# Graph keys at a stride of 32 rows: V placed by copies, silu from the exponential

## Chip, cores and metric

The kernel runs on one core of a Trainium2 chip. The metric is the device time of one execution in microseconds (us). Engines: PE multiplies matrices (PEld is its weight load), DVE, ACT and POOL work on 128 partitions by element, SP only issues transfers. Everything is float32.

## What is computed

32 batches of 32 tokens of 128 features go through a transformer layer with modulation from a condition, and then through a graph attention layer in two directions. Cut to what matters:

```python
cmod = silu(c) @ w_ada + b_ada                     # 6 vectors of 128 for each batch
x_mod = ln(x) * (1 + scale_msa) + shift_msa
k, q, v = split(x_mod @ w_qkv)                     # 16 heads of 8
y = softmax((q / 8) @ k.T) @ v
x = x + gate_msa * (y @ w_proj + b_proj)
x = x + gate_mlp * (gelu(ln_mod(x) @ w_mlp1 + b_mlp1) @ w_mlp2 + b_mlp2)
# the graph layer: 32 queries, but only the first 20 tokens as keys
self_feat = concat(x, c or 0) @ W_self.T + b_self
for d in range(2):                                 # the adjacency as it is, and swapped
    A = adj if d == 0 else swapaxes(adj, 1, 2)
    aff = q1[d] @ k1[d].T / sqrt(8)                # masked by A.sum(-1) > 0
    w = softmax(aff + A @ w_bias + b_bias)         # over 20 keys, 16 heads
    output += (w @ self_feat[:, :20]) through Wout[d] + bout[d]
out = x + relu(self_feat + output)
```

## The kernel before

The kernel is a list of steps, `ORDER`, each a pair of stage and key. `ON` gives each its engine and `BANKS` each PSUM tile its bank of four (`ps_b0` to `ps_b3`); the scores have four banks of their own (`ps_s`). Each engine runs its steps in the list's order (`mine`), and before each waits for the steps that it needs (`fresh`). The order stands in the file as a table, and a step that waits holds back all behind it on its engine.

A unit is a group of four batches (128 query rows) and, in the graph layer, a direction: 8 units in the first layer, 16 in the graph layer. Sets of one or two units share softmax steps (`SETS`); the graph layer has eight sets of two (sets 5 to 12). The dense products go by chunks (`CHUNKS`, first layer up to the attention) or by four mids of eight batches (`MIDS`). A set passes through these stages:

- `scores` (L1030, PE): for each batch and each of four row strips j of the features a product of 32 queries with four heads' keys. K stands in `Kb0` or `Kb1` once for each of the four heads of a strip, masked by `head_mask` (`take` of k on ACT, L1101; `k1mask`, L755, on POOL or DVE, into a ring of two mids).
- `badd` (L1355, DVE, graph layer alone): adds the edge bias, PSUM to `E1`. `max` and `sub`: the row maximum of each head, and its subtraction (L1379 on DVE in the first layer, L723 on DVE or POOL in the graph layer). `E0` has a ring of two, `E1` of three sets.
- `turn` (L1041 graph, L1044 first layer, PE): transposes E of a unit, so that keys stand on partitions. The graph layer has 16 x 20 = 320 key columns, padded to 360 with -30000 by the step `zero pad`, in three parts of six heads x 20 keys (120 rows). The first layer has 16 x 32 = 512 columns in four parts of 128.
- `exp` (L1173 or L1176, ACT): exp from PSUM into `PT`, a ring of four units.
- `values` (L1066 or L1074, PE): for each part and batch a product of `PT` with V. V is block-diagonal: in `Vz1` a head's 20 rows hold its 8 columns and a column of ones (which yields the denominator), the rest zeros. `recip` and `mult` (L1388, L1399, DVE) divide. `ya` adds the two directions, `oT` turns back, `fin1`, `fin2` and `store` end the work.

V of the graph layer comes from the product `v1` (L989: only the 20 key rows of each batch) and a DVE transposition of 32 x 32 blocks (L1262) into `v1_raw`, where the keys of four heads stand at partitions 0, 32, 64 and 96. From there `spread_half` (L779) moves them by DMA to partitions at a stride of 20: 8 transfers a mid, 32 in all, 20 issued by SP and 12 by ACT. In the first layer `vmask` (L745) builds `Vz0` by multiplying with `quad_mask`.

The start: x is loaded in three parts, statistics on DVE (L1200, L1203), with epsilon added in L1206, the power -1/2 on POOL (L855), the scaled x on ACT or DVE (`apply`), its transposition on PE (`xnT`) and the modulation on DVE and POOL (`take` xnT and `shift`). `silu` (L1137) is one ACT step, after which the table for exp is loaded; the first `cmod` product waits for it and for its weights. PE runs 11 transpositions of `ident` first (`WARM`) and pairs of them in three `warm` steps.

Of the kernel before, what the change touches and what calls it, by code (L numbers as in the profile page):

```python
# [5 lines left out]
ALU = mybir.AluOpType  # L6
# [5 lines left out]
P = 128  # L12
B = 32
# [11 lines left out]
SIX = 6  # L25
CH = 3
CW = C + 1
UW = H * CW
KR = SIX * M
EW = CH * KR  # L30
# [21 lines left out]
SPREAD_PARTS = [[(0, 0, 0, 0, CH), (1, 1, 0, 0, CH), (4, 0, CH, 0, 1), (4, 1, CH, 1, 1)],  # L52
                [(2, 2, 0, 0, CH), (3, 3, 0, 0, CH), (5, 2, CH, 0, 1), (5, 3, CH, 1, 1)]]

# [16 lines left out]
WARM = 11  # L71
# [4 lines left out]
 'bhead': 'pool',  # L76
# [6 lines left out]
 'fin2': 'dve',  # L83
 'gbias': 'dve',
 'ident': 'pool',
 'k1mask': 'pool',
# [14 lines left out]
 'spread': 'sp',  # L101
 'stats': 'dve',
 'store': 'sp',
 'sub': 'pool',
 'turn': 'pe',
 'values': 'pe',
 'vmask': 'pool',
 'warm': 'pe',
 'ya': 'pool',
 'zero': 'pool',  # L110
 ('apply', 0): 'dve',
 ('bhead', 0): 'act',
 ('k1mask', (0, 1)): 'dve',
 ('k1mask', (1, 1)): 'dve',
 ('resid1', 2): 'dve',
 ('resid1', 3): 'dve',
 ('resid2', 2): 'pool',
 ('shift', (0, 0)): 'dve',
 ('shift', (0, 2)): 'dve',
 ('shift', (1, 2)): 'dve',  # L120
 ('spread', ('v1', 1, 0)): 'act',
 ('spread', ('v1', 2, 1)): 'act',
 ('spread', ('v1', 3, 1)): 'act',
 ('sub', 0): 'dve',
 ('sub', 1): 'dve',
 ('sub', 2): 'dve',
 ('sub', 3): 'dve',
 ('sub', 4): 'dve',
 ('sub', 7): 'dve',
 ('take', (('cmod', 0), 0)): 'dve',  # L130
 ('take', (('cmod', 1), 0)): 'dve',
 ('take', (('k', 0), 0)): 'act',
# [19 lines left out]
 ('take', (('k1', 0, 0), 0)): 'act',  # L152
 ('take', (('k1', 0, 1), 0)): 'act',
 ('take', (('k1', 1, 0), 0)): 'dve',
 ('take', (('k1', 1, 1), 0)): 'dve',
 ('take', (('k1', 2, 0), 0)): 'dve',
 ('take', (('k1', 2, 1), 0)): 'act',
 ('take', (('k1', 3, 0), 0)): 'act',
 ('take', (('k1', 3, 1), 0)): 'dve',
# [31 lines left out]
 ('take', (('q1', 1, 0), 0)): 'dve',  # L191
# [88 lines left out]
 ('turn', 12): 0,  # L280
# [1182 lines left out]
```

## Time and profile before

| what | us |
|---|---|
| median of 3 runs | 95.89 |
| lowest, highest | 95.29, 96.32 |
| the profiled execution | 96.85 |
| its span, first to last instruction | 95.1 |

Busy of the span are PE 87%, weight loads 69%, DVE 75%, POOL 52% and ACT 44%. The whole has 4068 recorded instructions, of which 1773 are PE products and transpositions and as many are weight loads: a float32 product is recorded as two products and two loads, a transposition as one of each. "Issue" in the chain or as a releaser is time in which an engine waited for nothing that the profile shows. The mean granted clock of PE is 0.982.

### The profile page before, as it was taken

The numbers are of one execution on the slowest core, as the hardware profiler recorded it, in microseconds if no ns is written. First come the engines' busy times: TensorE is split into PE (matmuls) and PEld (weight loads), VectorE is DVE, ScalarE is ACT, GpSimd is POOL, SyncE is SP. The second block draws the span as 40 slices with busy tenths as digits, with TensorE's granted clock in tenths as the row PEclk, the third lists the DMA queues.
The fourth block names the chain that finished last, engine by engine and source line by source line (L and its number), as shares of the span: only waits on it lengthen the run. The fifth ranks groups of instructions, "written<-read, shape, count | busy, mean of one in ns | idle before, by whom it ended". The sixth has DMA issues, their size and how long they took to land.

```text
span 95.1 us, 4068 instructions
## 1 busy us (share of the span) xinstructions
PE 82.7 (87%) x1773; PEld 65.6 (69%) x1773; DVE 71.7 (75%) x181; ACT 41.8 (44%) x96; POOL 49.0 (52%) x60
## 2 busy tenths in 40 slices
PE   3867999799999698999999999999999874998910
PEld 3745789567666386888878788788788763787700
DVE  3397477978796986888875999869788953689790
ACT  0928424977820488617066028731254221307300
POOL 4252439999976423239720541044995918263310
PEclk9999999999999999999999999999999999759999
DMA  1899991000000000000001100001110030020303
GB/s 35 263 317 277 422 405 64 0 0 7 3 7 7 0 3 7 0 0 0 7 0 30 38 10 0 7 0 21 24 41 8 16 70 6 21 57 16 110 7 110
DMA packets 3890, 5.75 MB, mean 60 GB/s; under 512 B 704, under 2 KB 3008, under 8 KB 3744
## 3 DMA queue, kind: packets, MB, share of 16 engines
q1 hardware_dynamic: 2840, 4.68, 15.3%
q10 hardware_dynamic: 1032, 0.80, 2.9%
q8 instruction: 14, 0.23, 1.0%
q14 instruction: 4, 0.03, 0.1%
HBM read 4.22 MB, written 0.52 MB: 50 GB/s over the span
## 4 chain that ended last, share of the span: by engine, by line
PE 74%; DVE 7%; issue 7%; ACT 4%; DMA 3%; POOL 1%; POOLq 1%; SPq 0%; ACTq 0%
PE ps_s L1030 12%; PE ps_b L971 7%; PE ps_b L945 7%; PE ps_b L965 7%; PE ps_b L894 5%; PE ps_b L1041 5%; PE ps_b L1066 5%; PE ps_b L1044 4%; PE ps_b L982 4%; PE ps_b L978 4%; DMA w_ada_sb<-in_w_ada 3%; PE ps_b L984 3%; PE ps_b L1074 2%; PE ps_b L921 2%; PE ps_b L953 2%
## 5 line engine op out<-in xcount | busy, mean ns | idle before, releaser
L1173 ACT ACTIVATE PT<-ps_b 120x384 f32<-120x384 f32 x16 | 7.2, 489 | 15.0 <-PE ps_b L1041 15.0
L755 POOL TENSOR_TENSOR Kb<-k_raw,head_mask 128x640 f32<-128x640 f32 x6 | 7.7, 1293 | 9.1 <-DVE k_raw L1273 4.7
L855 POOL TENSOR_TENSOR rstd<-var_eps,minus_half 128x2 f32<-128x2 f32 (+1 forms) x9 | 6.0, 671 | 8.6 <-DVE var_eps L1206 8.5
L723 POOL TENSOR_TENSOR E<-E,neg_max 128x640 f32<-128x640 f32 x7 | 8.9, 1271 | 0.9 <-DVE neg_max L1363 0.8
L1116 ACT ACTIVATE hidden<-ps_b,cols 128x256 f32<-128x256 f32 x16 | 7.1, 476 | 4.7 <-PE ps_b L965 4.7
L945 PE MATMUL ps_b<-xm,w_qkv_sb 128*128 128x256 f32 (+1 forms) x30 | 8.6, 418 | 0.0
L965 PE MATMUL ps_b<-xm,w_rest_sb 128*128 128x256 f32 x32 | 8.4, 381 | 0.0
L1066 PE MATMUL ps_b<-Vz,PT 120*32 120x54 f32 (+1 forms) x384 | 6.6, 216 | 2.1 <-issue 2.1
L1066 PEld LDWEIGHTS ps_b<-Vz,PT 120*32 120x32 f32 (+1 forms) x384 | 5.5, 116 | 4.0 <-issue 3.4
L1101 ACT ACTIVATE Kb<-ps_b,head_mask 128x256 f32<-128x256 f32 (+1 forms) x20 | 7.3, 440 | 1.9 <-PE ps_b L945 1.8
L1030 PE MATMUL ps_s<-Kb,home_b 32*32 32x80 f32 x512 | 8.0, 251 | 0.0
L745 POOL TENSOR_TENSOR Vz<-v_raw,quad_mask 128x1152 f32<-128x1152 f32 (+1 forms) x4 | 7.5, 1866 | 0.9 <-DVE v_raw L1238 0.9
L1355 DVE TENSOR_TENSOR E<-ps_s,bias_head 128x640 f32<-128x640 f32 x8 | 6.6, 823 | 1.7 <-PE ps_s L1030 1.5
L707 POOL TENSOR_TENSOR xm<-xm,cmod 128x256 f32<-128x256 f32 (+1 forms) x6 | 4.2, 705 | 7.1 <-DVE xm L1228 7.1
L971 PE MATMUL ps_b<-hidden,w_rest_sb 128*128 128x256 f32 x32 | 7.7, 382 | 0.0
L1388 DVE RECIPROCAL rden<-ps_b 128x32 f32<-128x32 f32 (+1 forms) x13 | 4.2, 330 | 4.2 <-PE ps_b L1066 3.3
L1041 PE MATMUL ps_b<-ident,E 128*120 128x128 f32 x48 | 6.9, 280 | 0.3 <-ACT PT L1173 0.3
L1030 PEld LDWEIGHTS ps_s<-Kb,home_b 32*32 32x32 f32 x512 | 5.9, 107 | 1.8 <-issue 1.4
L1368 DVE TENSOR_REDUCE neg_max<-ps_s 128x32 f32<-128x1024 f32 (+1 forms) x5 | 5.1, 1011 | 2.1 <-PE ps_s L1030 2.1
L728 POOL TENSOR_TENSOR home_a<-home_a 128x128 f32<-128x128 f32 x6 | 2.6, 455 | 7.7 <-DVE home_a L1399 5.7
L965 PEld LDWEIGHTS ps_b<-xm,w_rest_sb 128*128 128x128 f32 x32 | 5.7, 190 | 1.1 <-issue 0.3
L971 PEld LDWEIGHTS ps_b<-hidden,w_rest_sb 128*128 128x128 f32 x32 | 5.9, 190 | 0.9
(109 smaller groups left out, 190.9 us busy)
## 6 DMA issues: line engine op xcount, KB each, us to landing
w_rest_sb<-in_w_rest SPq DMA_DIRECT2D x1, 1088.0 KB, 9.8
home_a<-in_adj SPq DMA_DIRECT2D x2, 448.0 KB, 6.4
home_a<-in_adj SPq DMA_DIRECT2D x1, 512.0 KB, 7.8
xT<-in_xT SPq DMA_DIRECT2D x1, 512.0 KB, 10.6
out<-gated SPq DMA_DIRECT2D x4, 128.0 KB, 1.8
Vz<-v_raw SPq DMA_DIRECT2D x10, 33.8 KB
x_tok<-in_x_tok ACTq DMA_DIRECT2D x1, 256.0 KB, 4.5
w_ada_sb<-in_w_ada SPq DMA_DIRECT2D x1, 256.0 KB, 7.9
```

The costliest lines, as they stand in the source:

```text
L723: return engine.tensor_tensor(e, e, less_max(key), ALU.add)
L745: return engine.tensor_tensor(Vz0[:, :, bs, :, :].rearrange("p i b j w -> p i (b j w)"), v0_raw[:, bs, :, :].rearrange("p b j w -> p (b j ...
L755: return engine.tensor_tensor(Kb1[:, m % K1_RING, d, :, 0:(g1 - g0) * UB, :].rearrange("p i b k -> p i (b k)"), k1_raw[:, d, bs, :].rearra ...
L945: return pe.matmul(ps[:, 0:n], w, xm[:, bs, :], start=True, stop=True)
L965: return pe.matmul(ps[:, 0:n], w_mlp1_sb[:, name[2], :], xm[:, bs, :], start=True, stop=True)
L971: ins = pe.matmul(ps[:, 0:n], w_mlp2_sb[:, j, :], hidden[:, h % HID_RING, j, 0:n], start=(j == js[0]), stop=(j == js[-1]))
L1030: ins = pe.matmul(ps_s[QUAD * b:QUAD * b + QUAD, j, u * nk:(u + 1) * nk], qT, Kb, start=True, stop=True)
L1041: ins = pe.transpose(ps[0:KR, c * P:(c + 1) * P], E1[:, r, u, c * KR:(c + 1) * KR], ident[:, :])
L1066: ins = pe.matmul(ps[QUAD * b:QUAD * b + QUAD, o + c * SIX * CW:o + c * SIX * CW + w], PT[0:rows, r, c, b * S:(b + 1) * S], V, start=True, ...
L1101: return act.activation(Kb0[:, part, bs, :], ps_bs, ACT.Copy, scale=head_mask[:, 1, part:part + 1])
L1116: return act.activation(hidden[:, h % HID_RING, j, 0:n], ps[:, 0:n], ACT.Gelu_apprx_tanh, bias=cols[:, R_MLP1 + j:R_MLP1 + j + 1])
L1173: ins = act.activation(PT[0:KR, r, 0:CH, :], ps[0:KR, 0:CH * P].rearrange("p (j t) -> p j t", t=P), ACT.Exp)
```

## The change

- Every head's keys in the graph layer take 32 rows: `E1` is now laid out as `E0`, [ring, 4 strips, 2 units, 4 heads, 32 keys], and the step `pad` fills columns 20 to 31 of each head, once. `turn` and `exp` of a graph unit thus handle four parts of 128.
- `v1` computes all 32 rows. After the same DVE transposition, four heads' keys already stand at the partitions that they need. A new step `vput` copies one quadrant of 32 partitions (32 x 576) from `v1_raw` to `Vz1`, 16 times in all, on POOL (9) and ACT (7). `spread_half` and its 32 transfers go. `values` has four parts of four heads, 16 products of 36 columns for 12 of 54 or 36. `Wout` is arranged on the host to match.
- Silu is computed as c / (1 + exp(-c)): exp on ACT (the table for exp is loaded first, no other follows), and a new step `gate_c` of three operations on DVE. The epsilon of the norms is added by POOL, ahead of the power.
- `WARM` is 13, and there are 16 `warm` steps of one transposition.
- `ORDER`, `ON` and `BANKS` are new tables. On DVE are now 3 of 8 graph subtractions (1 before) and 4 of 8 `k1mask` steps (2 before).

```diff
-SIX = 6
-CH = 3
-KR = SIX * M
-EW = CH * KR
-WARM = 11
+WARM = 13
- 'bhead': 'pool',
+ 'bhead': 'act',
+ 'gate_c': 'dve',
- 'k1mask': 'pool',
+ 'k1mask': 'dve',
- 'sub': 'pool',
+ 'sub': 'dve',
+ 'vput': 'pool',
...
-        v1_raw = sb("v1_raw", [P, HJ, B, DIRS, CW])
-        Vz1 = sb("Vz1", [P, V1_RING, SIX, CH, NB1, DIRS, CW])
+        v1_raw = sb("v1_raw", [P, B, DIRS, HJ, CW])
+        Vz1 = sb("Vz1", [P, V1_RING, HI, NB1, DIRS, HJ, CW])
-        E1 = sb("E1", [P, E1_RING, 2, EW])
+        E1 = sb("E1", [P, E1_RING, HJ, 2, HI, S])
...
-            for i, quad, j, c, n in SPREAD_PARTS[half]:
-                engine.dma_start(Vz1[M * i:M * i + M, k, i, c:c + n, 0:nb, :, :].rearrange("p c b d w -> p c (b d w)"),
-                                 v1_raw[QUAD * quad:QUAD * quad + M, j:j + n, bs, :, :].rearrange("p c b d w -> p c (b d w)"))\
-                      .then_inc(spread_done["v1", m, half], 16)
+            q = slice(QUAD * i, QUAD * i + QUAD)
+            return (Vz1[q, m % V1_RING, i, 0:(g1 - g0) * UB, :, :, :].rearrange("p b d j w -> p (b d j w)"),
+                    v1_raw[q, bs, :, :, :].rearrange("p b d j w -> p (b d j w)"))
...
+                    wait_own(pool.tensor_scalar(var_eps[:, layer, g0:g1], meanvar[:, layer, g0:g1, 1], LN_EPS, None, ALU.add))
                     ins = pool.tensor_tensor(rstd[:, layer, g0:g1], var_eps[:, layer, g0:g1], minus_half[:, 0:g1 - g0],
                                              ALU.pow)
...
-                    ins = pe.matmul(to[:, :, d, 0:M], w_v1[:, d, :], selfT[:, bs, 0:M], start=True, stop=True)
+                    ins = pe.matmul(to[:, :, d, :], w_v1[:, d, :], selfT[:, bs, :], start=True, stop=True)
...
-                    for i in range(2):
-                        ins = pe.transpose(ps_s[:, i, 0:P], ident[:, :], ident[:, :])
+                    ins = pe.transpose(ps_s[:, key % HJ, 0:P], ident[:, :], ident[:, :])
...
-                        for c in range(CH):
-                            ins = pe.transpose(ps[0:KR, c * P:(c + 1) * P], E1[:, r, u, c * KR:(c + 1) * KR], ident[:, :])
+                    E = E1 if UNITS[key][0] else E0
+                    for j in range(HJ):
+                        ins = pe.transpose(ps[:, j * P:(j + 1) * P], E[:, r, j, u, :, :], ident[:, :])
...
-                    act.activation(silu_c[:, :], cols[:, R_COND:R_COND + B], ACT.Silu).then_inc(told(stage, key), 1)
-                    act.preload_act_table(ACT.Exp)
+                    ins = act.activation(silu_e[:, :], cols[:, R_COND:R_COND + B], ACT.Exp, scale=-1.0)
...
+                    wait_own(dve.scalar_tensor_tensor(out=silu_e[:, :], in0=silu_e[:, :], scalar=1.0, in1=silu_e[:, :],
+                                                      op0=ALU.add, op1=ALU.max))
+                    wait_own(dve.reciprocal(silu_r[:, :], silu_e[:, :]))
+                    ins = dve.tensor_tensor(silu_c[:, :], cols[:, R_COND:R_COND + B], silu_r[:, :], ALU.mult)
```

The graph layer on PE, in the stretch with both halts of the chain. Before (L1066 value products, L1030 scores, L1041 transpositions of E, L982, L984 and L989 the products q1, k1 and v1):

```order
L1066 MATMUL ps_b<-Vz,PT 32x54 x8
L1066 MATMUL ps_b<-Vz,PT 32x36 x4
L1030 MATMUL ps_s<-Kb,home_b 32x80 x32
L1066 MATMUL ps_b<-Vz,PT 32x54 x8
L1066 MATMUL ps_b<-Vz,PT 32x36 x4
L1066 MATMUL ps_b<-Vz,PT 32x54 x8
L1066 MATMUL ps_b<-Vz,PT 32x36 x4
L1041 MATMUL ps_b<-ident,E 120x128 x6
L1030 MATMUL ps_s<-Kb,home_b 32x80 x32
```

After, from the products q1 and k1 of the last mid on (L1062 value products, L1028 scores, L1040 transpositions, L981, L983 and L988 the products q1, k1 and v1):

```order
L983 MATMUL ps_b<-selfT,w_rest_sb 128x160
L981 MATMUL ps_b<-selfT,w_rest_sb 128x256
L983 MATMUL ps_b<-selfT,w_rest_sb 128x160
L1062 MATMUL ps_b<-Vz,PT 32x36 x32
L1028 MATMUL ps_s<-Kb,home_b 32x80 x32
L1040 MATMUL ps_b<-ident,E 128x128 x8
L981 MATMUL ps_b<-selfT,w_rest_sb 128x256
L988 MATMUL ps_b<-selfT,w_rest_sb 128x8x32 x2
L1062 MATMUL ps_b<-Vz,PT 32x36 x32
L1028 MATMUL ps_s<-Kb,home_b 32x80 x32
```

In before, two value sets (four units) stand around one score set, with only six transpositions behind; in the new order a score set, eight transpositions and products of 160 or 256 columns stand between one value set and the next.

The start on DVE, before (L1292 adds 1 to two bias columns, L1200 and L1203 are statistics, L1206 adds epsilon, L1218 takes the first modulation):

```order
L1292 SCALAR_TENSOR_TENSOR cols<-cols 128x1 x2
L1200 BN_STATS stats<-x_tok 128x6
L1203 BN_AGGR meanvar<-stats 128x2
L1206 SCALAR_TENSOR_TENSOR var_eps<-meanvar 128x1
L1200 BN_STATS stats<-x_tok 128x6 x2
L1203 BN_AGGR meanvar<-stats 128x2 x2
L1206 SCALAR_TENSOR_TENSOR var_eps<-meanvar 128x2
L1218 TENSOR_TENSOR cmod<-ps_b,cols 128x64
```

After (L1287 to L1290 are `gate_c`, L1302 the factor for ACT's share of the norm):

```order
L1274 SCALAR_TENSOR_TENSOR cols<-cols 128x1 x2
L1287 SCALAR_TENSOR_TENSOR silu_e<-silu_e 128x32
L1289 RECIPROCAL silu_r<-silu_e 128x32
L1290 TENSOR_TENSOR silu_c<-cols,silu_r 128x32
L1185 BN_STATS stats<-x_tok 128x6
L1188 BN_AGGR meanvar<-stats 128x2
L1185 BN_STATS stats<-x_tok 128x6 x2
L1188 BN_AGGR meanvar<-stats 128x2 x2
L1185 BN_STATS stats<-x_tok 128x6
L1188 BN_AGGR meanvar<-stats 128x2
L1185 BN_STATS stats<-x_tok 128x6 x2
L1188 BN_AGGR meanvar<-stats 128x2 x2
```

The three operations of `gate_c` stand ahead of all statistics, and four of the five chunks have their statistics ahead of the first modulation.

## Rows read from the trace of the kernel before

**Rows 1.** The page: busy time, share of the span, instructions.

```profile
PE 82.7 (87%) x1773; PEld 65.6 (69%) x1773; DVE 71.7 (75%) x181; ACT 41.8 (44%) x96; POOL 49.0 (52%) x60
```

**Rows 2.** Windows: length, busy PE, PEld, DVE, ACT, POOL (records), clock, DMA, GB/s.

```profile
9.50:34.80 25.30, 23.66 (x521) 17.72 (x521) 19.72 (x45) 13.83 (x39) 18.58 (x19) 1.00 0.22 86
...
55.40:75.10 19.70, 19.70 (x555) 16.58 (x554) 16.81 (x31) 9.09 (x20) 10.80 (x9) 1.00 0.06 14
56.39:84.99 28.60, 26.48 (x778) 21.79 (x779) 22.29 (x40) 10.44 (x23) 15.56 (x15) 0.94 0.10 22
75.10:80.80 5.70, 3.59 (x170) 2.75 (x163) 3.14 (x6) 0.87 (x2) 3.45 (x5) 1.00 0.16 35
80.80:85.40 4.60, 4.59 (x128) 3.67 (x128) 3.31 (x7) 0.87 (x2) 2.02 (x3) 0.63 0.16 40
```

**Rows 3.** The chain that ended last: start, us, what.

```profile
9.90 1.71 PE ps_b L945 x4
...
13.71 1.00 PE ps_s L1030 x56
...
29.22 0.18 issue
...
33.47 1.35 PE ps_b L1044 x12
...
45.54 0.43 PE ps_b L978 x2
...
59.84 0.84 PE ps_s L1030 x49
...
71.07 0.80 PE ps_b L1041 x6
...
72.14 1.12 PE ps_b L989 x8
...
75.76 0.85 issue
...
79.54 1.26 issue
...
81.87 1.14 PE ps_s L1030 x59
```

**Rows 4.** Windows from the start to each of the two halts.

```profile
0.00:75.76 75.76, 70.29 (x1354) 55.85 (x1355) 59.50 (x155) 37.45 (x86) 41.94 (x51) 1.00 0.20 63
0.00:79.54 79.54, 73.22 (x1481) 58.10 (x1482) 61.76 (x159) 38.32 (x88) 43.72 (x54) 1.00 0.20 63
```

**Rows 5.** DMA queue (packets, MB, share): whole span, then 78.2 to 78.3.

```profile
q8 instruction: 14, 0.23, 1.0%
...
q8 instruction: 1, 0.02, 74.4%
```

**Rows 6.** Groups of instructions by form: busy us, mean ns, idle before.

```profile
L1173 ACT ACTIVATE PT<-ps_b 120x384 f32<-120x384 f32 x16 | 7.2, 489 | 15.0 <-PE ps_b L1041 15.0
...
L1176 ACT ACTIVATE PT<-ps_b 128x512 f32<-128x512 f32 x8 | 4.5, 596 | 0.7 <-PE ps_b L1044 0.7
...
L755 DVE TENSOR_TENSOR Kb<-k_raw,head_mask 128x640 f32<-128x640 f32 x2 | 1.7, 860 | 0.1
...
L883 POOL COPY bias_head<-bias_dir 128x640 f32<-128x640 f32 x1 | 0.7, 717 | 0.0
```

**Rows 7.** Timeline of PE: value products, the first graph scores, the last values.

```profile
35.66 1.36 PE L1074 MATMUL ps_b<-Vz,PT 128*32 128x36 f32 x128
...
55.44 0.91 PE L1030 MATMUL ps_s<-Kb,home_b 32*32 32x80 f32 x64
...
88.53 1.25 PE L1066 MATMUL ps_b<-Vz,PT 120*32 120x54 f32 x96
```

**Rows 8.** Timeline of the start, silu and the first modulation product.

```profile
3.52 0.23 ACT L1137 ACTIVATE silu_c<-cols 128x32 f32<-128x32 f32 x1
...
4.50 1.06 PE L921 MATMUL ps_b<-silu_c,w_ada_sb 128*128 128x32 f32 x4 [0.30 <-DMA w_ada_sb<-in_w_ada]
```

More of the change, by code:

```diff
@@ L628, in done @@
                 return ld[key], 16
-            if stage == "spread":
-                return spread_done[key], 16 * len(SPREAD_PARTS[key[2]])
             engine = engine_of(stage, key)
@@ L722, in subtract1 @@
             e = e1_heads(key)
-            return engine.tensor_tensor(e, e, less_max(key), ALU.add)
+            less = max_of(key).unsqueeze(3).broadcast_to([P, HJ, len(SETS[key]) * HI, M])
+            return engine.tensor_tensor(e, e, less, ALU.add)
         def add_dirs(engine, name, g):
@@ L806, in _ @@
             for stage, key in mine("sp"):
-                if stage == "spread":
-                    spread_half(sp, "sp", *key[1:])
-                else:
-                    assert stage == "store"
-                    g0, g1 = FINS[key]
-                    for s in fresh("sp", ("fin2", key)):
-                        sp.wait_ge(*s)
-                    sp.dma_start(out[:, g0 * P:g1 * P], outT[:, g0 * UB:g1 * UB, :].rearrange("p b s -> p (b s)"))\
-                      .then_inc(stored, 16)
+                assert stage == "store"
+                g0, g1 = FINS[key]
+                for s in fresh("sp", ("fin2", key)):
+                    sp.wait_ge(*s)
+                sp.dma_start(out[:, g0 * P:g1 * P], outT[:, g0 * UB:g1 * UB, :].rearrange("p b s -> p (b s)"))\
+                  .then_inc(stored, 16)
             sp.wait_ge(stored, 16 * len(STORES))
@@ L827, in wait_own @@
                 pool.wait_ge(own, count[0])
+            before = None
             for stage, key in mine("pool"):
+                if before is not None and "vput" in (stage, before[0]):
+                    for s in fresh("pool", before):
+                        pool.wait_ge(*s)
+                before = (stage, key)
                 if stage == "ident":
@@ L874, in _ @@
                     ins = spread_k1(pool, "pool", *key)
+                elif stage == "vput":
+                    for s in fresh("pool", ("take", (("v1", key[0]), 0)), ("zero", f"vz1{key[0] % V1_RING}"),
+                                   ("zero", "v1_ones"), *v1_home_read(key[0])):
+                        pool.wait_ge(*s)
+                    ins = pool.tensor_copy(*v1_block(*key))
                 elif stage == "adjf":
@@ L917, in dense_product @@
                 if kind == "cmod":
[L918 removed]
+                    for s in fresh("pe", ("load", f"ada{name[1]}"), ("gate_c", 0)):
                         pe.wait_ge(*s)
@@ L1129, in take_part @@
                                       bias=bk_scaled[:, d:d + 1], scale=C ** -0.5)
+            act.preload_act_table(ACT.Exp)
             for stage, key in mine("act"):
@@ L1328, in _ @@
                     ins = spread_v(dve, "dve", key)
+                elif stage == "vput":
+                    for s in fresh("dve", ("take", (("v1", key[0]), 0)), ("zero", f"vz1{key[0] % V1_RING}"),
+                                   ("zero", "v1_ones"), *v1_home_read(key[0])):
+                        dve.wait_ge(*s)
+                    ins = dve.tensor_copy(*v1_block(*key))
                 elif stage == "k1mask":
```

512 lines of the change are left out of this document (247 added, 265 removed), and 7 rows, old and new, of the table ORDER.

## Prediction, made before the changed kernel was run

> **What bounds the kernel now.** I read the engines' busy shares first, then the windows by stage, then the chain that ended last, and last the places where the chain has "issue". The shares say PE: 82.7 of 95.1 us, and PE is busy in all of 55.4 to 75.1 [rows 1, 2]. From the first q and k product (9.7 us) to the last value product (89.8 us [rows 7]) its queue is the spine of the program; outside that stand the start and a tail of 5.3 us (normalise, add the directions, transpose, add, store). The reader is to see where this spine loses time without working:
> - 75.1 to 80.8: PE is busy 3.59 of 5.70 us. The chain has two halts there, 0.85 us at 75.76 and 1.26 us at 79.54, both "issue", and both in the middle of a group of value products [rows 2, 3]. A wait for a transfer of V would stand before a group's first product; these don't. Up to the first halt PE has 1354 + 1355 products and weight loads behind it, up to the second 1481 + 1482: 254 more [rows 4]. A small halt (0.18 us at 29.22) stands in the middle of a score group [rows 3]. The queue of instruction transfers has 14 packets of together 0.23 MB; one crosses at 78.2 us, 2.6 us before PE goes on (79.54 + 1.26) [rows 3, 5]. So I read the halts as PE's code arriving late: one block for some 256 of its instructions, requested when the block before is entered, and PE here runs through a block faster than the next comes. This case's trace thus differs from the Trainium skill ("Runtime: NRT & Kernel Launch", section on instruction fetch mechanics), which has the same blocks of 256 instructions but calls the cost of crossing from one to the next mostly hidden; the sum goes by the halts in the rows.
> - 80.8 to 85.4: the granted clock is 0.63 [rows 2]; 59 score records take 1.14 us where 49 take 0.84 at full clock, and it follows the two halts [rows 3]. By the chain's rows against the same groups elsewhere this costs about 1.4 us.
> - 9.7 to about 14: 4 product records take 1.71 us, 0.43 each, where a record of the same size later takes 0.215 [rows 3]. That is the lower of the two clock levels, although the clock column reads 1.00. PE had worked and paused in turns before. Some 4.4 us of work at half rate cost 2.2 us.
>
> **The change part by part.**
> *Turning E in the graph layer.* 48 transpositions of 120 columns become 64 of 128. The chain has 6 in 0.80 us, 0.133 each; back to back in the first layer 12 take 1.35, 0.113 each [rows 3]. 16 more are 1.8 to 2.1 us, on the path. Take +1.9.
> *v1 product.* 8 products (16 records) move 256 keys for 160. 8 records of 160 take 1.12 us, 0.14 each; a record of 256 takes 0.215 [rows 3]. 16 x 0.078 = +1.3.
> *Value products.* 12 a unit (54, 54 and 36 columns) become 16 of 36, as in the first layer. There 4 units take 1.36 us, here 1.25 [rows 7]; 16 units make +0.4.
> *Exp.* 512 columns for 384: 0.596 for 0.489 us [rows 6], 16 times +1.7 on ACT, which is busy 9.1 of the 19.7 us from 55.4 [rows 2]. Hidden, save 0.1 in the last link.
> *Placing V.* 32 transfers go, no wait of PE shows for them, so I credit nothing; had one been on the path it would show ahead of a value group. 16 copies of 32 x 576 come, 9 on POOL, 7 on ACT. No row has 32 partitions. Nearest above: a copy of 128 x 640 on POOL, 0.72 us; nearest below: exp of 120 x 384 on ACT, 0.49 [rows 6]. I take 0.65: 5.9 us on POOL, 4.6 on ACT, behind PE's work as long as the copies for groups 2 and 3 are done some 11 us after the first graph scores; in POOL's order they are through after about 6. If that cover were gone, each would cost its 0.65.
> *Layer norm's epsilon on POOL.* Nine small operations move from DVE to POOL, where no row has them alone; beside the other engines' work they cost nothing, at most the 0.2 or so of one on the way to the first norm, which is in the start below.
> *Masks and subtractions.* Two of the graph subtractions and two key maskings (0.86 us on DVE [rows 6]) move to DVE. Between the first bias add and the last maximum DVE is busy 22.3 of 28.6 us [rows 2]; by my count of its new order about 26. This is near PE's own need. The ring of E still has three places, and the fifth bias add waits for the turns of the second set, where DVE will stand about 1 to 2 us; PE has other work then. I put nothing for it, and 1.5 us as the upper bound.
> *Silu.* One of two table switches at the start goes. Exp would end at 3.75 as silu does now [rows 8], and three small DVE operations with waits between follow, between 0.5 and 1.1 us; I take 0.75. The first modulation product starts at 4.50 now, released by its weights [rows 8], so it hardly moves. But these operations stand ahead of all statistics in DVE's queue, which holds the first statistics until 4.5 us; adding up DVE, POOL and ACT from there, the first q and k product starts at 9.9, 0.2 later.
> *Warming.* 13 transpositions at the start for 11, and 16 single ones for 6. They fill PE's pauses up to the first product. If the full rate is there when it starts, up to 2.2 us are won; but the fourth part of chunk 4's norm (on ACT) now stands before the copies of K that the first scores need. Adding up ACT's queue, these scores end at 14.05 instead of 14.71 [rows 3]. Bounds 0 and -2.2; I take -1.0 (the 0.65 and a little shorter stretch to the graph layer).
> *Code blocks.* PE gets 312 more instructions (64 products of four, 28 transpositions of two), a fifteenth block. The halts stood where value groups and scores follow each other with little between. Laid over the new order, blocks in the graph layer come 3.2 to 3.6 us of pure PE work apart, for 1.6 to 2.4 at the halts now. So the halts go, and with them the low clock: -2.1 - 1.4 = -3.5. Spacings near the time that a block needs (from the end of the first halt to the end of the second, 76.61 to 80.80, are 4.2 us [rows 3]) leave small halts: +0.5 in all, bounds 0 and +3.5.
> *Tail.* The last addition moves to DVE, -0.2; the last exp is longer, +0.1. The last DVE chain is otherwise the same.
> Sum: 1.9 + 1.3 + 0.4 - 1.0 - 3.5 + 0.5 = -0.4. The profiled execution took 96.85 us around its span of 95.1 and would take 96.45; the median of the runs shown is 95.89, so I forecast 95.5.
>
> **The rivals.**
> *A, PE keeps its pace.* The full rate is there from the first product and no block is late. Then -2.2 stands for -1.0 and no +0.5: -2.1, 93.8 us. For it: pages evenly spaced, hardly a pause left in PE's first 10 us. Against it: ACT, DVE and POOL, busy 14, 20 and 19 us in the 25 us from 9.5 [rows 2], would have to follow a faster PE.
> *B, the code sets the pace (slower).* From the block entered in the first value group of the graph layer to the end there are now six entries for five. If every block costs the 3.9 to 4.2 us between entry and use, the stretch from the first graph scores to the last value product takes 12.4 + 6 x 3.9 + 1.0 = 36.8 us; now it takes 34.3 (55.44 to 89.78 [rows 7]). With the start's -0.7 that is +1.8: 97.7 us. It decides from a spacing of less than 3.9 us on. For it: the sixth entry comes of the change itself, and the new spacings are below 3.9. Against it: waits for DVE between them stretch them anyway, and in before blocks of 4.0 us show no halt.
> *C, the halts are a wait for V after all.* Then their removal is certain, and with all else as above the sum is -0.9: 95.0 us. Against it is their place in the middle of groups [rows 3, 4].
> *D, a copy of V or DVE comes late.* The 1.5 us of DVE's bound fall on the path: +1.1, 97.0 us. It decides when the turns of the second set end after 17 us from the first graph scores; a clock that falls in the new pause would add to it.
>
> **How the numbers follow.** The forecast has 0.40, A 0.28, B 0.17, C 0.04, D 0.11. About 1% is what a measurement of this kernel tells from no change. The forecast's own spread is 94.5 to 96.5 and puts 0.29 within 1%, 0.08 faster and 0.03 slower; A and part of C are faster, B and D slower or, at their lower edge, the same. Faster 0.37, same 0.34, slower 0.29. The range runs to just beyond A and to B: 93.6 to 97.7.
>
> **What would show it.** Right: no "issue" over 0.4 us among the value products, granted clock 1.00 from 75 us to the last product; 15 instruction packets on PE's queue; 8 transpositions in 0.9 to 1.05 us; first scores over by 14.1. Wrong: halts again in the middle of groups some 256 instructions apart, longer in sum than 0.5 us (B); the bias add of the fifth set late and PE idle behind it (D); value groups that wait for the copies; or 0.215 us a record from the first q product and the graph layer's first scores before 54 us (A). If the copies of 32 partitions take 1 us or more, the term for placing V fails.

## The result, and the profile after

The changed kernel takes 102.66 us (median of 4 runs, 101.89 to 106.26); the kernel before took 96.10 beside it. The ratio is 1.066, 95% interval 1.054 to 1.079: slower by some 6.5 us, where 95.5 us were forecast and 97.7 was the end of the range. The profiled execution took 102.34 us around a span of 100.5.

The kernel before scatters, from 94.8 to 98.6 us over all runs below; a median is given of all runs of a kernel, while the ratios and their intervals leave out the runs that lie over 1.5% above its fastest. By these the kernel before took 95.5, 95.65 and 96.3 us in the three sets of runs. So the experiments are compared by their ratio to the runs of before beside them, and two of one set also directly.

The page of the changed kernel: busy shares, the clock column and the queue of instruction transfers.

```profile
PE 85.7 (85%) x1929; PEld 68.4 (68%) x1929; DVE 74.6 (74%) x177; ACT 48.6 (48%) x105; POOL 54.4 (54%) x74
...
PEclk9999999958999999999999999999999999999995
...
q8 instruction: 15, 0.25, 1.1%
```

PE has 3.0 us more of busy time than before [rows 1], and the span is 5.4 us longer: the rest is idle time. The windows say where. Their columns are those of [rows 2].

```profile
9.50:34.80 25.30, 22.59 (x502) 16.70 (x504) 17.86 (x38) 13.44 (x37) 17.11 (x21) 0.93 0.23 88
59.70:79.40 19.70, 19.70 (x585) 16.13 (x584) 16.52 (x29) 9.38 (x19) 10.57 (x11) 1.00 0.01 4
79.40:85.10 5.70, 5.70 (x232) 4.71 (x219) 5.66 (x10) 2.96 (x7) 4.61 (x5) 1.00 0.02 6
```

The second and third row answer to the 19.7 us from the first graph scores, where PE was and is busy throughout, and to the stretch with the two halts, where it now is, at full clock. The first row answers to the first layer: 502 records for 521 in the same time, PE idle for 2.7 us for 1.6, and the clock at 0.93. So the gain and the loss lie in different stages. By the first layer's and the graph layer's scores and the last value product in the timelines:

| us | before | after | difference |
|---|---|---|---|
| start to the end of the first scores | 14.71 | 13.97 | -0.7 |
| from there to the first graph scores | 40.73 | 45.73 | +5.0 |
| from there to the end of the last value product | 34.34 | 35.5 | +1.2 |
| from there to the end of the span | 5.3 | 5.3 | 0.0 |

In the second of these stretches PE is busy 38.58 of 40.73 us before and 40.41 of 45.73 after: 3.2 us more of idle time, and 1.8 us more of busy time for the same number of products.

The list of PE's waits (what was waited for, us in total, times, longest) names the middle stretch:

```profile
PE ps_b L893 <- ACT xn_tok L1096: 2.9, 2, 1.5
PE ps_b L893 <- ACT selfT L1083: 2.1, 1, 2.1
PE ps_s L994 <- POOL ident L825: 1.8, 1, 1.8
PE ps_b L893 <- DVE home_a L723: 1.7, 1, 1.7
PE ps_b L893 <- ACT xn_tok L1140: 1.4, 2, 1.2
```

L893 is the line of PE's transpositions other than those of E. Three waits ahead of normalised chunks make 4.9 us: 2.05 at 15.24, 1.55 at 35.82 and 1.31 at 52.2. The releasers named are ACT's, but each time ACT had waited for the small factor `nmr` from DVE. The timeline of the first of them (start, us, engine, line, operation, what it writes and reads):

```profile
13.99 1.23 DVE L1360 TENSOR_REDUCE neg_max<-ps_s 128x32 f32<-128x1024 f32 x1
14.04 2.11 POOL L740 TENSOR_TENSOR Vz<-v_raw,quad_mask 128x1152 f32<-128x1152 f32 x1 [0.23 <-DVE v_raw L1220]
15.13 1.03 DVE L1302 SCALAR_TENSOR_TENSOR nmr<-meanvar,rstd 128x2 f32<-128x2 f32 x1
16.09 1.21 DVE L1369 TENSOR_TENSOR E<-ps_s,neg_max 128x1024 f32<-128x1024 f32 x1
16.20 0.88 ACT L1140 ACTIVATE xn_tok<-x_tok,nmr,rstd 128x128 f32<-128x128 f32 x2 [2.59 <-DVE nmr L1302]
...
17.29 0.33 PE L893 MATMUL ps_b<-ident,xn_tok 128*128 128x128 f32 x1 [2.05 <-ACT selfT L1083]
```

`nmr` has two values a row and takes 0.12 to 0.15 us elsewhere. Here it stands behind the first score maximum, and then takes 1.03 us: it ends with POOL's masking of V (16.15). In the kernel before it stood ahead of that maximum, and PE had two more groups of products in front of the transposition. After the idle time the clock falls (0.51 from 19.8 to 22.8 us, 1.00 again from 25 us on): at 19.91 eight transpositions take 1.90 us, where the graph layer's take 1.02.

```profile
19.91 1.90 PE ps_b L1040 x8
```

The end of the chain, value products to the last DVE chain (start, us, what):

```profile
93.23 0.69 PE ps_b L1062 x55
93.91 0.51 issue
94.42 0.53 PE ps_b L1062 x33
94.95 0.02 issue
94.97 0.37 DVE rden L1378
```

One halt of 0.51 us is left of the halts of [rows 3].

### The profile page after: what moved, and what is told of

Same layout as the page of the kernel before. It is cut to its first block, busy times and chain, and to the rows that moved or that the text cites. A ratio compares the mean times of both kernels' runs of the same rounds, so it can differ in the third digit from the quotient of the medians.

```text
span 100.5 us, 4367 instructions
## 1 busy us (share of the span) xinstructions
PE 85.7 (85%) x1929; PEld 68.4 (68%) x1929; DVE 74.6 (74%) x177; ACT 48.6 (48%) x105; POOL 54.4 (54%) x74
## 4 chain that ended last, share of the span: by engine, by line
PE 67%; DVE 14%; ACT 6%; DMA 5%; issue 4%; ACTq 1%
PE ps_s L1028 10%; PE ps_b L1040 9%; PE ps_b L970 7%; PE ps_b L1062 7%; PE ps_b L964 6%; PE ps_b L893 5%; DMA x_tok<-in_x_tok 5%; PE ps_b L944 4%; PE ps_b L977 4%; PE ps_b L910 3%; PE ps_b L981 3%; PE ps_b L988 3%; PE ps_b L983 2%; PE ps_b L952 2%; ACT xn_tok L1140 2%
## 5 line engine op out<-in xcount | busy, mean ns | idle before, releaser
L1161 ACT ACTIVATE PT<-ps_b 128x512 f32<-128x512 f32 x24 | 13.6, 596 | 14.2 <-PE ps_b L1040 14.0
L1040 PE MATMUL ps_b<-ident,E 128*128 128x128 f32 x96 | 14.6, 291 | 0.0
L1040 PEld LDWEIGHTS ps_b<-ident,E 128*128 128x128 f32 x96 | 11.3, 148 | 1.3 <-DVE cmod L1200 0.2
L1062 PEld LDWEIGHTS ps_b<-Vz,PT 128*32 128x32 f32 x768 | 8.0, 109 | 3.7 <-issue 2.6
L1062 PE MATMUL ps_b<-Vz,PT 128*32 128x36 f32 x768 | 9.6, 199 | 0.8 <-issue 0.5
L750 POOL TENSOR_TENSOR Kb<-k_raw,head_mask 128x640 f32<-128x640 f32 x4 | 5.1, 1282 | 7.7 <-ACT k_raw L1115 3.9
L893 PE MATMUL ps_b<-ident,xn_tok 128*128 128x128 f32 x16 | 3.5, 290 | 6.3 <-ACT xn_tok L1096 2.9
L873 POOL COPY Vz<-v_raw 32x576 f32<-32x576 f32 x9 | 7.8, 869 | 1.7 <-DVE v_raw L1244 1.2
L893 PEld LDWEIGHTS ps_b<-ident,xn_tok 128*128 128x128 f32 x16 | 1.8, 140 | 8.4 <-issue 4.2
L1028 PE MATMUL ps_s<-Kb,home_b 32*32 32x80 f32 x512 | 7.3, 239 | 0.0
L1140 ACT ACTIVATE xn_tok<-x_tok,nmr,rstd 128x128 f32<-128x128 f32 x8 | 3.4, 483 | 7.6 <-DVE nmr L1302 7.6
L1028 PEld LDWEIGHTS ps_s<-Kb,home_b 32*32 32x32 f32 x512 | 5.3, 103 | 2.0 <-issue 1.2
L1356 DVE TENSOR_REDUCE neg_max<-E 128x32 f32<-128x640 f32 x8 | 6.5, 815 | 0.2
```

Source lines behind the costliest of these rows:

```text
L873: ins = pool.tensor_copy(*v1_block(*key))
L893: ins = pe.transpose(ps[:, i * P:(i + 1) * P], src(i), ident[:, :])
L1028: ins = pe.matmul(ps_s[QUAD * b:QUAD * b + QUAD, j, u * nk:(u + 1) * nk], qT, Kb, start=True, stop=True)
L1040: ins = pe.transpose(ps[:, j * P:(j + 1) * P], E[:, r, j, u, :, :], ident[:, :])
L1062: ins = pe.matmul(ps[QUAD * b:QUAD * b + QUAD, o + j * HI * CW:o + (j + 1) * HI * CW], PT[:, r, j, b * S:(b + 1) * S], V, start=True, stop ...
L1161: ins = act.activation(PT[:, r, :, :], ps[:, :].rearrange("p (j t) -> p j t", t=P), ACT.Exp)
```

## The experiments

Twelve kernels in three sets of runs (1 to 4, 5 to 8, 9 to 12). `ORDER` is the table from which every engine's queue is made. An entry matters only by its place among those of its own engine: in runs 1, 2, 5 and 11 DVE's queue alone differs from that of the kernel they start from, in runs 6 and 12 PE's alone.

**1. The last norm of the first layer ahead of the first maximum.**

```diff
- ('scores', 2), ('max', 2), ('rstd', (0, 3)), ... ('nmr', (0, 3)), ('apply', 3),
+ ('scores', 2), ('rstd', (0, 3)), ('nmr', (0, 3)), ('max', 2), ... ('apply', 3),
```

> The changed kernel, with the last chunk's norm of the first layer (rstd on POOL, nmr on DVE) written ahead of the first score maximum instead of behind it; nothing else. In the changed kernel PE stands idle for 2.05 us from 15.24 us, until the last norm (nmr at 15.13, which took 1.03 us for 0.15) has been applied by ACT (16.20 to 17.08), and afterwards the granted clock falls (8 transpositions in 1.90 us at 19.91). Theory 1, the order of the first layer is what made the change slower: nmr ends before 13.5, the halt goes, and with it the low clock, the first graph scores start at 56.2 to 57.7 for 59.70, and the kernel takes 99 to 100.5 us for 102.7. Rival 1, ACT or DVE hold the next step anyway (the copies of K, sub of the first scores): the halt only moves behind the next wait, and the time stays within 0.7 us of 102.7. Rival 2, the clock falls whatever the halt: some 1.5 to 2 us are won and the window from 20 to 25 us keeps a clock under 0.95.

Measured: 99.89 us (98.85 to 101.16), ratio to before 1.042 (1.030 to 1.055), some 2.8 us less than the changed kernel. `nmr` takes 0.12 us, the idle time of 2.05 is gone (the transpositions follow the work ahead without a pause), the clock column reads 9 up to the last slice, and from the first scores to the graph's it takes 42.4 us for 45.7. PE is busy 39.17 us of them for 40.41, so 2.1 of the 3.3 us are idle time and 1.2 are the low clock that is gone too. Theory 1 holds; the first graph scores at 58.8 miss its 57.7 because in this profile the input landed 0.9 us late and the first scores ended at 16.4.

**2. Two norms of the second layer norm put ahead as well.**

```diff
- ('rstd', (1, 1)), ('sub', 3), ... ('pen', 0), ('nmr', (1, 1)),
+ ('rstd', (1, 1)), ('nmr', (1, 1)), ('sub', 3), ... ('pen', 0),
- ('take', (('mlp2', 0), 0)), ... ('rstd', (1, 2)), ... ('resid2', 0), ('bhead', 0), ('nmr', (1, 2)),
+ ('rstd', (1, 2)), ('nmr', (1, 2)), ('take', (('mlp2', 0), 0)), ... ('resid2', 0), ('bhead', 0),
```

> As the run before it (the last norm of the first layer ahead of the first maximum), and two norms of the second layer norm put ahead in DVE's order: nmr of the second chunk ahead of the subtraction that stands before it (PE idle 1.55 us at 35.82), nmr of the third chunk ahead of the gating, a query copy and a residual (PE idle 1.31 us at 52.2). Theory 1, these waits are on the path: another 2.0 to 2.8 us, so 96.5 to 98.5 us in all. Rival, DVE and ACT are then late with other copies: under 1 us beside the run with the first norm alone.

Measured: 96.96 us (95.69 to 98.55), ratio 1.007 (0.999 to 1.015). Three small operations with two values a row each, moved in one engine's queue, give back 5.7 us of the 6.5 (by the ratios too: 1.007 for 1.066). PE's longest waits, start and tail included:

```profile
PE ps_s L995 <- POOL ident L826: 1.8, 1, 1.8
PE ps_b L894 <- DVE home_a L724: 1.7, 1, 1.7
PE ps_b L894 <- ACT xn_tok L1141: 1.2, 2, 1.0
```

The waits for the second layer norm's chunks (L1096 above) are gone; line numbers are one higher here. The chain still shows 6 us of DVE from 78.9 to 84.9, as in the changed kernel from 84.4 to 90.4. But PE is busy 5.8 of these 6.0 us and has no pause over 0.3: the chain went through the other of two queues that were equally full.

**3. The new structure in the old order.**

```diff
- ORDER, ON, BANKS, WARM of the changed kernel
+ those of the kernel before; ('spread', ('v1', m, h)) -> ('vput', (m, 2h)), ('vput', (m, 2h + 1)); ('gate_c', 0) behind ('silu', 0)
```

> The changed kernel's structure (keys at 32 rows, copies for V, silu through the exponential, epsilon on POOL) in the order, on the engines and in the PSUM banks of the kernel before; each pair of transfers is replaced by two copies on POOL or ACT where it stood. Theory 1, the new order lost the time, the structure costs only what the sum said (+3.6 of PE's work and at most the halts of code): 96.5 to 99 us, the first graph scores within 0.8 us of the 55.4 of before. Rival, the structure itself costs it (the masks' and the norm's operations on POOL, copies of V beside DVE): the first graph scores come after 57.5 us and the time is 101 us or more.

Measured: 99.20 us (98.90 to 100.31), ratio 1.043 (1.031 to 1.055). The first graph scores come at 56.30, 0.86 later than the 55.44 before; both numbers are a little beyond theory 1's and far from the rival's. Against the 95.5 us of before in this set it is 3.7 us. The terms give 4.2: +3.6 of PE's work, -0.3 since the halts are shorter (0.56 and 0.54 in the fence below and a third of 0.66 at 90.75, 1.8 for 2.1), and 0.9 from start and middle. The stretch from the first graph scores to the last value product is 35.77 us; the same terms give 34.34 - 3.5 + 1.8 + 3.6 = 36.2. Both sums are 0.4 to 0.5 us too high. So in the order of before the new structure costs 3.7 us. Chain and windows of this kernel, in two fences:

```profile
80.11 0.56 issue
...
82.75 0.67 PE ps_s L1031 x39
83.42 0.54 issue
83.96 0.48 PE ps_s L1031 x20
```

```profile
0.00:80.11 80.11, 74.12 (x1481) 58.43 (x1482) 62.96 (x152) 40.59 (x91) 50.32 (x69) 1.00 0.17 55
0.00:83.42 83.42, 76.87 (x1609) 60.61 (x1609) 65.05 (x156) 41.69 (x93) 52.90 (x73) 1.00 0.16 53
```

The halt at 80.11 has 1481 + 1482 records behind it, exactly as in the kernel before [rows 4], though other instructions stand there (the halt falls into a group of scores); the next has 255 more. The third has 1862 + 1862.

**4. The kernel before without its transfers of V.** Placing V is left out, its home is filled with ones.

```diff
- engine.dma_start(Vz1[...], v1_raw[...]).then_inc(spread_done["v1", m, half], 16)
- for s in fresh("pe", ("spread", ("v1", m, 0)), ("spread", ("v1", m, 1))):
+ for s in fresh("pe", ("take", (("v1", m), 0)), ("zero", f"vz1{m % V1_RING}")):
```

> The kernel before without its 32 transfers of V; the placing of V in the graph layer is left out, the home of V is filled with ones, and the value products read that. PE's instructions are the same in number and order. Theory 1 (the halts at 75.76 and 79.54 us are PE's code coming late): 'issue' of 0.6 to 1.4 us in the middle of value groups stays, behind the same number of products and weight loads (1354 + 1355 and 1481 + 1482). Rival (they are waits for V or come from the transfers' traffic): no issue above 0.4 us from 73 to 82 us, and 94.5 us or less.

Measured: 95.62 us in a single run, the two halts unchanged in place and count. Windows and chain:

```profile
0.00:75.49 75.49, 69.56 (x1354) 54.99 (x1355) 59.02 (x155) 37.39 (x86) 41.89 (x51) 1.00 0.18 58
0.00:79.23 79.23, 72.20 (x1481) 57.14 (x1482) 61.28 (x159) 38.26 (x88) 43.38 (x53) 1.00 0.17 56
80.00:85.00 5.00, 4.17 (x132) 3.08 (x131) 4.19 (x8) 1.34 (x4) 3.02 (x4) 1.00 0.02 5
```

```profile
75.49 1.10 issue
...
79.23 1.00 issue
```

The halts are not waits for V or its traffic. The third window shows something the prediction had joined to them: after the same halts the clock stays at 1.00 here, where it was 0.63 before [rows 2]. Run 8 has halts of 0.90 and 1.32 us at the same counts and keeps 1.00 behind them as well.

**5. The start in another order, on top of run 2.**

```diff
- ('gate_c', 0), ('stats', (0, 0)), ... ('stats', (0, 1)), ('stats', (0, 3)), ('nmr', (0, 0)), ... ('nmr', (0, 2)), ... ('take', (('cmod', 0), 0)),
+ ('stats', (0, 0)), ('gate_c', 0), ... ('stats', (0, 1)), ('nmr', (0, 0)), ... ('nmr', (0, 2)), ... ('take', (('cmod', 0), 0)), ('stats', (0, 3)),
```

> The changed kernel with the three norms ahead (as the second run of the first four) and its start put in another order on DVE: the first chunk's statistics ahead of the three small operations of the silu, and the norms of the first two chunks and the copy of the modulation ahead of the statistics that wait for the last load of x. Theory: these waits are on the way to the first q and k product, which moves from 10.3 us to 9.0 to 9.4, and with it everything behind it; the kernel takes 95.6 to 96.2 us where the run with the norms alone took 97.0. Rival: PE at full clock from its first product is then held by ACT's copies of K and by the norms of the last chunks, the first scores end less than 0.4 us earlier than 14.09, and the time stays at 96.6 to 97.2.

Measured: 95.39 us (94.59 to 96.43), ratio 0.996 (0.991 to 1.001). The first q and k product starts at 9.59 (0.2 later than expected), the first scores end at 13.2 for 14.09, and the time is 0.2 us below the range that was expected: theory. In the changed kernel the factors of the first two chunks stood behind statistics that waited for the last load of x, and `gate_c` ahead of statistics whose input was there.

**6. The tail.**

```diff
- ('turn', 16), ('exp', 18), ... ('turn', 17), ('exp', 16), ('dense', ('oT', 3)), ... ('values', 19), ('values', 16), ('values', 18), ('exp', 17), ('values', 17),
+ ('turn', 16), ('turn', 17), ('exp', 18), ('exp', 16), ('exp', 17), ... ('values', 19), ('values', 18), ('dense', ('oT', 3)), ... ('values', 16), ('values', 17),
```

> The run before it, and the last value group put in the order 19, 18, 16, 17 (for 19, 16, 18, 17), with the turns and exps for 16 and 17 ahead, so that normalising and adding set 10 can run beside the last two value units. Theory: from the last value product to the end it takes 4.9 to 5.1 us for 5.5, so 0.4 to 0.6 us less than the run before it. Rival: PE waits for the exps of 18 and 16 instead, and nothing is won.

Measured: 95.96 us (95.50 to 96.46), ratio 1.005 (0.999 to 1.011), half a microsecond more than run 5: a miss. From the last value product to the end it takes 5.75 us for run 5's 5.34, where 4.9 to 5.1 were expected. The timeline shows why the tail gained nothing:

```profile
86.50 0.33 PE L893 MATMUL ps_b<-ident,home_a 128*128 128x128 f32 x1
87.29 0.33 PE L893 MATMUL ps_b<-ident,home_a 128*128 128x128 f32 x1 [0.46 <-issue]
87.55 0.77 PE L1062 MATMUL ps_b<-Vz,PT 128*32 128x36 f32 x64
87.66 0.48 DVE L1401 SCALAR_TENSOR_TENSOR gated<-ps_b,bout_sum,selfT 128x256 f32<-128x256 f32 x1 [1.44 <-PE ps_b L893]
```

The halt now falls between the two halves of an output transposition (again 1862 + 1862 records behind it), and DVE, whose next piece waits for that transposition, stands for 1.44 us and only then normalises set 10. The rest of the half microsecond isn't placed: start and middle, where the order is the same, were 0.7 us longer in this profile too.

**7. The masking of V for the first scores' chunk off POOL**, in the changed kernel itself: `ON[('vmask', 2)] = 'dve'`, where it comes behind the first subtraction.

> The changed kernel, with the masking of V for the first scores' chunk (2.11 us on POOL from 14.04) on DVE, behind the first subtraction; the norms stand where they stood. Theory (a long tensor operation on POOL holds DVE up): nmr of the last chunk, behind the first maximum, takes 0.15 to 0.2 us for 1.03, and PE stands idle ahead of the last chunk's transpositions for 1.1 to 1.3 us for 2.05. Rival (nmr is long for another reason, as the maximum before it): it stays at 0.8 us or more and the idle time at 2 us.

Measured in a single run: 100.38 us. The same places in the timeline:

```profile
14.18 1.23 DVE L1361 TENSOR_REDUCE neg_max<-ps_s 128x32 f32<-128x1024 f32 x1
15.32 0.15 DVE L1303 SCALAR_TENSOR_TENSOR nmr<-meanvar,rstd 128x2 f32<-128x2 f32 x1
...
16.60 0.44 PE L894 MATMUL ps_b<-ident,xn_tok 128*128 128x128 f32 x2 [1.17 <-ACT selfT L1084]
```

0.15 us for 1.03 with nothing of POOL beside it, and 1.17 us of idle time for 2.05: theory, in both numbers. So of the 2.05 us some 0.9 are POOL's holding DVE up and 1.2 the place behind the maximum. The clock doesn't fall behind the shorter idle time (1.00 from 14 to 26 us), and from the first scores to the graph's it takes 43.6 us for 45.7: 0.9 of shorter idle time and 1.2 of full clock.

**8. The kernel before with the silu through the exponential alone** (`silu_e`, `gate_c` ahead of all statistics, one table).

> The kernel before with one part of the change alone: silu through the exponential, with its three small operations ahead of all statistics on DVE; all else, the warming and epsilon on DVE too, as before. Theory (they hold the statistics up until 4.5 us): the first q and k product comes 0.2 to 0.8 us later than 9.7 to 10.0 and the time is 0.2 to 0.8 us longer. Rival (the load of x paces the statistics, and a table switch less is won): the same or up to 0.3 us faster.

Measured: 96.96 us (96.82 to 98.51), ratio 1.015 (1.004 to 1.025): slower, by more than the expected 0.2 to 0.8 us at the middle of the interval and within it at its lower end. I read it so that the operations that come are on the path and the table switch that goes is not, but no run shows it: its profile cannot place the time, since there the first weights landed 1.3 us late.

**9. Epsilon back on DVE**, on top of run 5.

> The changed kernel with the norms and the start in the better order (the fifth run; 95.4 us, fast runs 95.2), with layer norm's epsilon back on DVE as in the kernel before (0.16 us a time for 0.22 on POOL and a hand-over). Theory, the epsilon on POOL costs next to nothing: within 0.3 us of 95.3. Rival, nine hand-overs of it are on the way of the norms: 0.4 to 1 us faster; or, the other way, DVE is late with it: 0.4 us or more slower.

Measured: 95.72 us (94.64 to 96.77) for 95.39, while the ratios to before, 0.992 (0.987 to 0.997) for 0.996, point the other way. No difference that these runs can tell; epsilon's move cost next to nothing.

**10. Without the copies of V**, on top of run 5. Placing V in the graph layer is left out, its home is filled with ones.

> The same kernel (norms and start in the better order) without its 16 copies of V: placing V in the graph layer is left out, its home is filled with ones and the value products read that, with the same number and shape of products. Theory, the copies (12.6 us of POOL and ACT) lie beside PE's work: within 0.4 us of 95.3, and the graph maskings on DVE take 0.86 to 0.95 us instead of up to 1.16. Rival, they hold DVE, the masks or the value groups up: 0.6 to 1.5 us faster.

Measured: 95.21 us (94.54 to 96.26) for 95.39; ratio 0.989 (0.985 to 0.993). That is 0.2 us by the times and 0.7 by the ratios of the two sets; run 9 of its own set, which differs by the epsilon as well, is 0.5 above it. So the copies are hidden but for something between 0.2 and 0.7 us, which these runs can't pin down; within 0.4 was expected. They held DVE up, as the groups by form show; first run 5, then this one:

```profile
L750 DVE TENSOR_TENSOR Kb<-k_raw,head_mask 128x640 f32<-128x640 f32 x4 | 4.6, 1160 | 0.0
L718 DVE TENSOR_TENSOR E<-E,neg_max 128x640 f32<-128x640 f32 x3 | 2.9, 962 | 0.0
```

```profile
L747 DVE TENSOR_TENSOR Kb<-k_raw,head_mask 128x640 f32<-128x640 f32 x4 | 3.6, 913 | 0.0
L715 DVE TENSOR_TENSOR E<-E,neg_max 128x640 f32<-128x640 f32 x3 | 2.4, 807 | 0.0
```

A masking takes 0.25 us and a subtraction 0.16 us less without the copies. It works the other way too: in the changed kernel five of POOL's nine copies take 0.66 us and the four that start beside such a masking or subtraction 1.10 to 1.14.

**11. The same medicine for the kernel before**: its norm of the second chunk, beside which PE idles 0.92 us, ahead of a maximum.

```diff
- ('scores', 4), ('max', 4), ('rstd', (1, 1)), ('nmr', (1, 1)),
+ ('rstd', (1, 1)), ('scores', 4), ('nmr', (1, 1)), ('max', 4),
```

> The kernel before, with the norm of the second layer norm's second chunk written ahead of the maximum beside which it now takes 0.82 us (31.20; PE idle 0.92 us at 32.14). Theory, a small norm operation behind a long DVE one and beside a POOL one is a loss in this kernel too: 0.6 to 1.0 us faster than the kernel before. Rival, PE is then held by a block of its code or by the next turn: within 0.3 us.

Measured: 96.91 us (95.88 to 98.06), ratio 1.005 (1.001 to 1.010): slower, and neither theory had that. The timeline tells:

```profile
29.08 2.11 POOL L745 TENSOR_TENSOR Vz<-v_raw,quad_mask 128x1152 f32<-128x1152 f32 x1
29.15 2.05 DVE L1313 SCALAR_TENSOR_TENSOR nmr<-meanvar,rstd 128x2 f32<-128x2 f32 x1 [0.61 <-POOL rstd L855]
...
31.12 1.21 DVE L1368 TENSOR_REDUCE neg_max<-ps_s 128x32 f32<-128x1024 f32 x1
31.29 0.81 ACT L1108 ACTIVATE xn_tok<-ps_b,nmr,rstd 128x128 f32<-128x128 f32 x2 [5.34 <-DVE nmr L1313]
...
32.23 0.41 PE L894 MATMUL ps_b<-ident,xn_tok 128*128 128x128 f32 x2 [1.25 <-ACT xn_tok L1108]
```

`rstd` comes from POOL, and POOL's next operation starts at once: `nmr` meets it from its first moment and waits all of it out, 2.05 us, while the maximum, which could have run beside it (as at 13.99 above), now stands behind. A small operation put ahead is only ahead if no long POOL operation is.

**12. The tail again, on top of run 5**: both last turns, the output transposition ahead of the value groups, then values 19, 18, 16, 17.

```diff
+ ('turn', 16), ('turn', 17), ('exp', 18), ('exp', 16), ('exp', 17), ... ('dense', ('oT', 3)), ('values', 19), ('values', 18), ... ('recip', 10), ('mult', 10), ('ya', 5), ('values', 16), ('values', 17),
```

> The kernel with the norms and the start in the better order, and the end in this order on PE: both turns of the last set, the third output transposition, values 19, 18, 16, 17; set 10 is normalised beside values 16 and 17. Theory: the transposition does not stand between the value groups now, the last normalisation alone follows the last product, and the kernel takes 0.3 to 0.6 us less than 95.3 (94.7 to 95.0). Rival, as in the sixth run: a halt of code (0.3 to 0.5 us of issue) or the wait for the output transposition takes it back, and it takes 95.3 to 95.9.

Measured: 95.07 us (94.55 to 95.80), 0.3 less than run 5 and 0.65 less than run 9 of its own set, and 0.990 of the kernel before (0.985 to 0.994). It lies just above the 94.7 to 95.0 of the theory. Its profile has no halt behind 1862 + 1862 records, and the end behind the last value product takes 5.18 us for run 5's 5.34. Its PE is busy 24.95 of the 25.3 us of the first layer's window, for 22.59 in the changed kernel:

```profile
9.50:34.80 25.30, 24.95 (x604) 18.00 (x606) 18.85 (x42) 15.53 (x42) 18.41 (x23) 1.00 0.24 90
```

## Why the prediction was wrong

It was right where it worked through rows, and wrong in the one stretch of 40 us that it did not work through.

- *The failing step* is "I take -1.0 (the 0.65 and a little shorter stretch to the graph layer)", bounds 0 and -2.2. The 0.65 came: the first scores end at 13.97, forecast 14.05. The stretch behind them was to be a little shorter and was 5.0 us longer: 3.2 us of idle time, 1.2 of the low clock behind the first wait (the difference in busy time to runs 1 and 7, 40.41 for 39.17), 0.6 of other busy time. No wait of the new order behind the first scores was looked for, and the bound above was put at nothing, as if a new order could only give. Runs 1 and 2 took 5.7 us of the time back by moving three `nmr`; with them, the stretch is 39.5 us, 1.2 less than before. So the "little shorter" is in the order too, under three waits.
- *"Beside the other engines' work they cost nothing"* was said of epsilon on POOL, and run 9 bears that out. But in the same queues stood what each norm needs, and its place was not followed.
- *Contention of DVE and POOL* was in no term. The trace of before had it: the same `nmr` at 31.20 took 0.82 us beside the masking of V, a row that was not read. Runs 7 and 11 show it. It made 0.9 us of the idle time and, by run 7's profile, the low clock behind it; that it was missed matters less than the order, since run 1 takes both away by the order alone.
- *Turns, v1, values* (+1.9, +1.3, +0.4): the graph layer's 64 transpositions at 1.02 us for eight make 8.2 us for 6.4 before (+1.8); 16 records of 256 keys at 0.215 make 3.4 for 2.2 (+1.2); a set of two units takes 0.70 for half of 1.25, eight times (+0.6). Together +3.6, the forecast's sum; run 3's stretch in the graph layer fits it to 0.4 us.
- *Halts and clock* (-2.1, -1.4, +0.5 for new ones): the two long halts are gone, one of 0.51 us came, the clock is 1.00 from 25 us on. The stretch from the graph's first scores to the last value product was to change by about +0.6 (3.6 - 3.5 + 0.5) and changed by +1.2. The size of the 1.4 us was right (PE is busy 31.97 us in this stretch before, and 30.53 for the same products in run 4 at clock 1.00); what failed is the link: runs 4 and 8 have the halts without the low clock, run 11 has both. So the 1.4 us was certain for the profiled execution of 96.85 us alone, and the forecast took it off the median of 95.89 in full. How many of the other runs had the low clock isn't known.
- *Rival A* (full rate from the first product) came in its first half: the first four q and k records take 1.10 us for 1.91. But PE then waited for the other engines, and 0.7 us of its 2.2 came; its other sign, graph scores before 54 us, came only with the norms moved (53.6 in run 2, 52.2 in run 5).
- *Rival C* (a wait for V) fell with run 4. *Rival B* (code sets the pace) did not come: there is one halt without a releaser, of 0.51 us, a little over the 0.4 that were named as the sign. *Rival D* seems at first sight to be there, since the chain runs over DVE for 6 us; PE was busy beside it, so it cost nothing.
- *Placing V at 0.65 us a copy* fits a copy alone (0.66 on POOL, 0.68 on ACT); POOL's mean is 0.87 since four of nine met a DVE operation, which is the contention again. By run 10 all but 0.2 to 0.7 us of it was hidden.
- *Silu*: `gate_c` took 0.81 us (forecast 0.75), and its place ahead of the statistics was named. The first q and k product started at 10.15 for the 9.9 forecast. Run 8 shows that this part alone costs more than the 0.2 us put down, and run 5 that the place can be mended.
- *Tail*: 0.0 for -0.1.

With the order mended (run 12) the whole is 1% under the kernel before, where -0.4 us was forecast. That isn't the price of the structure: run 12 had its order worked on in three places, while the kernel before had one such try (run 11), which failed. In the order of before the structure costs 3.7 us (run 3), and what it is worth with the best order for each isn't shown.

## What to carry to other kernels

A change that rewrites the order of a whole program is two changes. Price the new operations from rows, but also walk the new order for every small value that a long chain needs (here a factor of two numbers a row): what stands ahead of it on its engine, and what PE still has to do until it is used. When a chain of waits runs over an engine for a while, look whether PE is idle there before that engine is blamed.

## What the runs showed of the hardware

- DVE's `nmr`, which reads two operands from SBUF, stood still while POOL masked V, which reads SBUF. It ended within 0.02 us of POOL's end in three kernels: 1.03 us in the changed one, 0.82 in the kernel before, 2.05 in run 11, and 0.15 when POOL was free (run 7). In the changed kernel it also took 0.15 us at 52.33, beside a POOL memset of 2.02 us, which only writes. The maximum beside the masking, which reads PSUM, took its usual 1.23 us. The Trainium skill has this in "SBUF — State Buffer", section "Who interferes with whom": "A DVE instruction with two SBUF inputs contends with a GpSimd instruction that reads SBUF". The trace agrees. On the length, these rows show that the one that started second was held up until the first had ended, POOL's copies by DVE's maskings too (1.10 to 1.14 us for 0.66).
- PE's long halts without a releaser stand at fixed counts of its instructions, whatever those are: behind 1354 + 1355 and 1481 + 1482 records in the kernel before and in runs 4, 8 and 11, behind 1481 + 1482 in run 3 too, and behind 1862 + 1862 in the changed kernel and in runs 1, 2, 3, 5, 6 and 7, even where that falls between the halves of one output transposition (1864 in run 10). Their length ran from 0.19 (run 1) to 1.32 us (run 8), and runs 9 and 12 have none there. That they are code arriving late is the reading of the prediction: run 4 excludes V's transfers, and the fixed counts speak for it, but no run varied the code's loading, and what sets their length isn't shown.
- After nearly equal halts the granted clock fell in the profiles of before (0.63 from 80.8 to 85.4 us) and of run 11 (0.72 from 80 to 86), and not at all in those of runs 4 and 8. In the changed kernel it fell to the lower level behind 2.05 us of idle PE, and not in run 7 behind 1.17 us. In the changed kernel's profile the low clock made 1.2 us of PE's busy time. Yet another execution of the changed kernel, with a mean clock of 0.997, took 101.89 us against 102.34 at 0.972: most of the loss is there without the low clock.
